# Relu attention pass: rounds written out, the mask added on VectorE, high key parts written by ScalarE and full keys by VectorE from one bank

## The reference

```python
def _L1_xattn_ref(input, context, context_mask, W, b):
    q = jax.nn.relu(jnp.einsum('bih,oh->bio', input, W) + b)
    k = jax.nn.relu(jnp.einsum('bjh,oh->bjo', context, W) + b)
    scores = jnp.einsum('bid,bjd->bij', q, k)
    scores = jnp.where(context_mask[:, None, :], -jnp.inf, scores)
    probs = jax.nn.softmax(scores, axis=2)
    return jnp.einsum('bij,bjd->bid', probs, k)
```

## Time and profile before

| what | value |
|---|---|
| three runs | 1555.84, 1556.08, 1556.17 us |
| the profiled execution | 1554.04 us, its span from first to last instruction 1552.3 us |
| TensorE busy | 1461.3 us (94%), weight loads 1258.2 us |
| VectorE, ScalarE, GpSimd busy | 1080.9, 828.1, 604.7 us |
| granted TensorE clock, mean | 0.975 |

### The profile page before, as it was taken

How to read it: one execution, slowest core, us unless ns; L and a number is a source line. 1 busy time by engine, 2 the same in 40 slices (tenths; PEclk the granted TensorE clock), 3 DMA queues, 4 the chain that set the end, 5 groups by cost and what they waited for, 6 DMA issues and landing times. The chain is left out here.

```text
span 1552.3 us, 24869 instructions
## 1 busy us (share of the span) xinstructions
PE 1461.3 (94%) x9105; PEld 1258.2 (81%) x9105; DVE 1080.9 (70%) x2053; ACT 828.1 (53%) x1578; POOL 604.7 (39%) x519
## 2 busy tenths in 40 slices
PE   6999999999999999999999999999977889999379
PEld 5888888888888888888888888888865778888248
DVE  6777777777777777777777777777775356666764
ACT  2655665556665565665565666565651255555121
POOL 6343433434343434343434343433300256665330
PEclk9999999999999999999999999999997899999779
DMA  5000000000000000000000000000007112220600
GB/s 183 1 8 18 1 25 1 25 1 25 1 25 1 25 1 25 1 24 1 24 1 24 1 24 1 1 1 1 1 28 312 63 70 71 71 71 24 284 1 4
DMA packets 9102, 57.18 MB, mean 37 GB/s; under 512 B 2121, under 2 KB 2720, under 8 KB 7969
## 3 DMA queue, kind: packets, MB, share of 16 engines
q1 hardware_dynamic: 8992, 55.73, 9.6%
HBM read 55.60 MB, written 0.13 MB: 36 GB/s over the span
## 5 line engine op out<-in xcount | busy, mean ns | idle before, releaser
L468 DVE TENSOR_TENSOR pT<-ps,pT 128x896 fp32r<-128x896 f32 x224 | 244.5, 1092 | 204.2 <-ACT pT L378 204.2
L305 POOL CAST V<-Vraw 128x512 fp32r<-128x512 f32 x189 | 115.8, 613 | 653.1 <-ACT Vraw L384 552.3
L378 ACT ACTIVATE pT<-ps 128x896 fp32r<-128x896 f32 x224 | 206.1, 920 | 179.1 <-PE ps L540 178.3
L384 ACT COPY Vraw<-ps 128x512 f32<-128x512 f32 x189 | 111.0, 587 | 265.3 <-PE ps L522 265.3
L306 POOL TENSOR_TENSOR V<-Vraw,V 128x512 fp32r<-128x512 f32 x189 | 242.3, 1282 | 15.1
L422 DVE TENSOR_REDUCE nmx<-ps 128x1 f32<-128x896 f32 x224 | 242.0, 1080 | 0.0
L365 ACT ACTIVATE prob<-ps,nm 128x896 f32<-128x896 f32 x224 | 224.2, 1001 | 0.0
L598 PE MATMUL ps<-ident,prob 128*128 128x128 f32 x1568 | 214.5, 277 | 8.6 <-ACT prob L365 4.5
L553 PEld LDWEIGHTS ps<-pT,V 128*128 128x128 f32 x1568 | 215.0, 188 | 8.3 <-issue 0.3
L553 PE MATMUL ps<-pT,V 128*128 128x256 f32 x1568 | 220.2, 280 | 0.0
L598 PEld LDWEIGHTS ps<-ident,prob 128*128 128x128 f32 x1568 | 167.5, 140 | 17.1 <-ACT prob L365 9.2
(11 more groups left out here) (307 smaller groups left out, 2398.6 us busy)
## 6 DMA issues: line engine op xcount, KB each, us to landing
raw<-in_ctxT SPq DMA_DIRECT2D x14, 896.0 KB, 4.5
d_raw<-in_ctxT SPq DMA_DIRECT2D x14, 896.0 KB, 4.6
w<-in_w SPq DMA_DIRECT2D x2, 4096.0 KB, 18.3
wg<-in_wg SPq DMA_DIRECT2D x1, 4352.0 KB, 27.5
wu<-in_wu SPq DMA_DIRECT2D x1, 4352.0 KB, 16.8
wd<-in_wd SPq DMA_DIRECT2D x1, 4352.0 KB, 26.7
e_ea<-in_alog SPq DMA_DIRECT2D x1, 2048.0 KB, 7.3
wq<-in_wq SPq DMA_DIRECT2D x1, 1024.0 KB, 5.3
```

Source lines behind the costliest of these rows:

```text
L305: link(pool, nc.gpsimd.tensor_copy(v_high(g, i), by_head(Vraw[:, j % 2, :])), "pool_chain")
L378: nc.scalar.activation(pT[u % 2][:, :, 0, :], pT_ps, ACT.Copy).then_inc(sem("pTh_ready"), 1)
L468: nc.vector.tensor_tensor(pT[u % 2][:, :, 1, :], pT_ps, pT[u % 2][:, :, 0, :].bitcast(F32), ALU.subtract).then_inc(sem("pTl_ready"), 1)
```

## The change

- The full keys are no longer ScalarE's. ScalarE writes the high part `d_kTh` straight from the bank, with bias and Relu (`keys`, `dkTh_ready`). VectorE then reads the same bank, adds the bias, takes the maximum with 0 and writes the full keys `d_kT` (`keys_full`, `dkT_ready`). The key groups' wait for their bank is still on `dkT_ready`, now VectorE's.
- The mask is loaded as 128 equal rows. VectorE adds mask times -1e30 to the scores as it reads them from the banks and writes `d_Sm` in SBUF; the maximum and the exponentials read `d_Sm`. The two mask products, `mneg` and the row of ones are gone.
- The scores of a half wait for the key parts of that half only, and go half by half.
- The high and low parts of the context and the full keys have two buffers each. Chunks 1 and 2 are both split ahead of round 0 (ScalarE) and in it (GpSimd), the others one round earlier than their keys, as before.
- The loops are gone: all 14 rounds are written out in each queue.
- `du_free` starts at 1, and `exp_step(c)` asks for c + 1.
- `wg` is allocated after the pass and loaded in `stage_scan`.

With `groups_ahead` = 4 the list `done` is 4, 8, ... 56, so each round still makes the four groups of the next chunk.

```diff
@@ -135,12 +135,14 @@
         keep("br1", [P, E1])
         with ExitStack() as experts:
 
-            v["wg"] = sb("wg", [P, KT, EA * F1], F32, experts)
             with ExitStack() as second:
 
-                v["d_raw0"] = sb("d_raw0", [P, KT, CK], F32, second)
-                for name, width in (("d_cTh", CK), ("d_cTl", CK), ("d_wxh", D), ("d_wxl", D)):
-                    v[name] = sb(name, [P, KT, width], F32R, second)
+                v["d_raw"] = [sb(f"d_raw{i}", [P, KT, CK], F32, second) for i in range(2)]
+                v["d_cTh"] = [sb(f"d_cTh{i}", [P, KT, CK], F32R, second) for i in range(2)]
+                v["d_cTl"] = [sb(f"d_cTl{i}", [P, KT, CK], F32R, second) for i in range(2)]
+                v["d_kT"] = [sb(f"d_kT{i}", [P, KT, CK], F32, second) for i in range(2)]
+                v["d_wxh"], v["d_wxl"] = (sb(name, [P, KT, D], F32R, second) for name in ("d_wxh", "d_wxl"))
+                v["early_groups"], v["early_splits"], v["early_loads"], v["groups_ahead"] = 0, 1, 1, 2 * KT
...
+            v["wg"] = sb("wg", [P, KT, EA * F1], F32, experts)
...
                 sp.dma_start(ea[:, :], t["alog"].partition_broadcast(P)).then_inc(sem("alog_in"), 16)
+                sp.dma_start(v["wg"][:, :, :], t["wg1"]).then_inc(sem("mix1_in"), 16)
                 sp.dma_start(v["wu"][:, :, :], t["wu1"]).then_inc(sem("mix1_in"), 16)
                 sp.dma_start(v["wd"][:, :, :], t["wd1"]).then_inc(sem("wd_in"), 16)
...
-    last = chunks // 2 - 1
+    KG = 2 * KT
+    NG = (NT + 1) // 2
+    groups = KG * chunks
+    early, split = v["early_groups"], v["early_splits"]
+    ahead = v["groups_ahead"]
+    done = [max(early, ahead)]
+    for c in range(chunks):
+        left = chunks - 1 - c
+        share = -(-(groups - done[-1]) // left) if left > 0 else 0
+        done.append(done[-1] + share)
+
+    def first_use(C):
+
+        return next((c for c in range(chunks) if done[c + 1] > KG * C), None)
+
+    to_split = {c: [C for C in range(chunks) if KG * C >= done[0] and max(first_use(C) - 1, 0) == c]
+                for c in range(chunks)}
...
+        Sm = sb("d_Sm", [P, 2, HK], F32, own)
...
+                def load_mask(c):
+                    if c >= 2:
+                        sp.wait_ge(sem("dmasked"), c - 1)
+                    sp.dma_start(mrow[c % 2][:, :], t["mask"][c].partition_broadcast(P)).then_inc(
+                        sem(f"dmask_in{c % 2}"), 16)
+
+                load_mask(0)
+                load_mask(1)
+                masks = 2
+                for C in range(v["early_loads"], chunks):
+                    if C >= 2:
+                        sp.wait_ge(sem("dcTl_ready"), C - 1)
+                    sp.dma_start(raw[C % 2][:, :, :], t["ctxT"][C]).then_inc(sem(f"dctx_in{C % 2}"), 16)
+                    if C >= 2 and masks < C - 1:
+                        load_mask(masks)
+                        masks += 1
+                for c in range(masks, chunks):
+                    load_mask(c)
...
+                def keys_low(c, g):
+                    pool.wait_ge(sem("dkT_ready"), KG * c + g + 1)
+                    nc.gpsimd.tensor_tensor(part(kTl, g), part(kT[c % ring], g), part(kTh, g).bitcast(F32),
+                                            ALU.subtract).then_inc(sem("dkTl_ready"), 1)
+
                 norm_pool(pool, 3)
+                for C in range(split, (done[0] + KG - 1) // KG):
+                    split_low(C)
                 for g in range(KG):
+                    keys_low(0, g)
+                for c in range(chunks):
+                    if c == 0:
+                        for C in to_split[0]:
+                            split_low(C)
+                    if c + 1 < chunks:
                         for g in range(KG):
+                            keys_low(c + 1, g)
+                    for C in to_split[c]:
+                        if c > 0:
+                            split_low(C)
 
...
-                def keys(g):
-                    nc.scalar.activation(part(kT, g), ps[:, g % 2, 0:HK], ACT.Relu, bias=bx[:, g // 2:g // 2 + 1],
-                                         scale=1.0).then_inc(sem("dkT_ready"), 1)
...
+                def keys(G):
+                    C, g = G // KG, G % KG
+                    act.wait_ge(sem("dk_done"), G + 1)
+                    if C >= 1:
+                        act.wait_ge(sem("ds_done"), C)
+                        act.wait_ge(sem("dkTl_ready"), KG * C)
+                    nc.scalar.activation(part(kTh, g), ps[:, G % 2, 0:HK], ACT.Relu, bias=bx[:, g // 2:g // 2 + 1],
+                                         scale=1.0).then_inc(sem("dkTh_ready"), 1)
+
+                def split_high(C):
+                    act.wait_ge(sem(f"dctx_in{C % 2}"), 16 * (C // 2 + 1))
+                    if C >= 2:
+                        act.wait_ge(sem("dk_done"), KG * (C - 1))
+                    nc.scalar.copy(cTh[C % 2][:, :, :], raw[C % 2][:, :, :]).then_inc(sem("dcTh_ready"), 1)
+
...
+                def exp_step(c):
+                    b = c % 2
+                    act.wait_ge(sem("dmax_done"), c + 1)
+                    act.wait_ge(sem("du_free"), c + 1)
+                    nc.scalar.activation(al[:, b:b + 1], nm[:, 1 - b:2 - b], ACT.Exp, bias=nm[:, b:b + 1], scale=-1.0)
+                    nc.scalar.activation(prob[:, :, :], Sm[:, :, :], ACT.Exp, bias=nm[:, b:b + 1], scale=1.0,
+                                         accum_out=rs[:, b:b + 1]).then_inc(sem("dexp_done"), 1)
 
...
+                for G in range(before, done[0]):
+                    keys(G)
+                for C in to_split[0]:
+                    split_high(C)
...
-                            act.wait_ge(sem("dmax_done"), i * 2 + (b + 2))
-                            act.wait_ge(sem("du_free"), i * 2 + (b + 2))
-                            exp_step(1 - b)
...
+                    for G in range(done[c], done[c + 1]):
+                        keys(G)
+                    if c > 0:
+                        for C in to_split[c]:
+                            split_high(C)
+                    for n in range(2):
+                        act.wait_ge(sem("dp_turned"), 2 * c + n + 1)
+                        nc.scalar.copy(pTh[:, turned_cols(n)], ps[:, 4 + n, 0:len(PG[n]) * P]).then_inc(sem("dpTh_ready"), 1)
+                    if c + 1 < chunks:
+                        for n in range(NG):
+                            rows_high(c + 1, n)
+                        exp_step(c + 1)
 
...
-                nc.vector.memset(nm[:, :], BIG).then_inc(sem("du_free"), 2)
+                nc.vector.memset(nm[:, :], BIG).then_inc(sem("du_free"), 1)
...
-                def keys_high(g):
-                    nc.vector.tensor_copy(part(kTh, g), part(kT, g)).then_inc(sem("dkTh_ready"), 1)
...
+                def keys_full(c):
+                    if c >= ring:
+                        dve.wait_ge(sem("dk_turned"), NG * (c - ring + 1))
+                        dve.wait_ge(sem("dkTl_ready"), KG * (c - ring + 1))
+                    for g in range(KG):
+                        G = KG * c + g
+                        dve.wait_ge(sem("dkTh_ready"), G + 1)
+                        nc.vector.tensor_scalar(part(kT[c % ring], g), ps[:, G % 2, 0:HK], bx[:, g // 2:g // 2 + 1], 0.0,
+                                                ALU.add, ALU.max).then_inc(sem("dkT_ready"), 1)
+
...
+                def masked_max(c):
+                    b = c % 2
+                    dve.wait_ge(sem(f"dmask_in{b}"), 16 * (c // 2 + 1))
+                    dve.wait_ge(sem("ds_done"), c + 1)
+                    if c >= 1:
+                        dve.wait_ge(sem("dexp_done"), c)
+                    nc.vector.scalar_tensor_tensor(Sm[:, :, :], mrow[b][:, :].rearrange("p (a n) -> p a n", a=2), -BIG, S,
+                                                   ALU.mult, ALU.add).then_inc(sem("dmasked"), 1)
+                    dve.wait_ge(sem("dmasked"), c + 1)
+                    nc.vector.tensor_reduce(nmx[:, :], Sm[:, :, :], mybir.AxisListType.XY, ALU.max,
+                                            negate=True).then_inc(sem("dchunk_max"), 1)
+                    dve.wait_ge(sem("dchunk_max"), c + 1)
+                    nc.vector.tensor_scalar(nm[:, b:b + 1], nmx[:, :], nm[:, 1 - b:2 - b], None,
+                                            ALU.min).then_inc(sem("dmax_done"), 1)
+
+                keys_full(0)
                 for n in range(NG):
                     rows_low(0, n)
...
+                def turn_keys(c, n):
+                    pe.wait_ge(sem("dkT_ready"), KG * (c + 1))
...
-                def scores(b, low_parts):
+                def scores(c):
                     halves = [slice(half * HK, (half + 1) * HK) for half in range(2)]
+                    if c >= 1:
+                        pe.wait_ge(sem("dmasked"), c)
                     for half, cols in enumerate(halves):
-                        nc.tensor.matmul(S[:, half, :], one_b[:, :], mneg[b][:, cols], start=True, stop=False)
```

(36 more changed lines are left out.)

307 lines of the change are left out of this document (94 added, 213 removed).

## The result

The changed kernel took 1575.11 us (median of four runs, 1572.84 to 1584.60), the kernel before 1556.12 us beside it (four runs, 1555.84 to 1556.85): a ratio of 1.0133 with a 95% interval of 1.0101 to 1.0164. It is slower, as forecast; the forecast was 1579 us. The profiled execution took 1572.84 us with a span of 1571.1 us, 18.8 us above the span before.

What follows compares the result with a forecast made beforehand. TensorE's order was taken to bound the kernel. Rounds 13.2, head 5.1 and tail 4.7 us sum to 23.0; 1554.04 + 23.0 + 2.04 gives 1579 us, range 1568 to 1594.

Steps and rivals of the forecast that it cites:

- x: Price of VectorE's write of full keys from the bank: between 0.37 and 1.23 us, taken as 0.61.
- twelve rounds more: Rounds of 14.82 us, 1.13 above 13.69; twelve give 13.6, less six loop ends of 0.07: 13.2 us.
- head: Start of the pass: round 0 begins 3.8 us late and takes 1.3 us more, 5.1 us in all.
- tail: End of the pass: 2.6 us waiting for the exponentials plus 2.1 us for an assumed half clock, 4.7 us.
- The bank's path: VectorE's full-key write now frees the bank; alone, scores at +7.57 against +7.64, gain eaten to 0.07 us a round.
- +6.35: Scores' start in a round without the two mask products and the wait before them: at most 1.29 us gained.
- The new wait: Exponentials wait for the present chunk's U update, ending at +2.73 in the next round; the round becomes 14.82 us.
- At nothing: Moved wg load, 128-row masks, GpSimd's low key parts, dmasked and the kT ring were to cost nothing.
- The rule on loops: Six loop ends at 0.07 us give 0.4 us; the skill's rule alone would have written-out rounds gain more.
- The wait did not hide: Rival: the exponentials' wait hides, rounds stay even, only head and part of the tail count: +5, 1561 us; chance 0.07.
- the clock kept 1.00: Rival: TensorE's clock falls every round because of its new idle gaps: +17, 1596 us; chance 0.13.
- the bank's write was not 0.37 us: Rival, faster: VectorE writes full keys at 0.37 us and U's wait hides: 1552 us; chance 0.05.

Runs made afterwards that it cites:

- a1: Changed kernel with du_free starting at 2 again, so the exponentials wait only for the U update of the chunk before: 1559.94 us, ratio 1.0032.
- c1: a2 with TensorE waiting for all four parts of d_kTh before the scores: 1550.91 us, ratio 0.9965.
- a2: Changed kernel with du_free at 2 again, ScalarE writing full keys from the bank and VectorE copying high parts: 1541.47 us, ratio 0.9917.
- a0: The changed kernel run once more, with no edit: 1574.63 us, ratio 1.0116 to the kernel before.
- d1: a1 with TensorE turning probabilities between second and third key groups, and the scores' high part before the first turning of keys: 1552.26 us.
- e2: d1 with ScalarE's and VectorE's copies of the turned probabilities also moved between the second and third group: 1547.42 us, ratio 0.9948.
- b1: Kernel before with only du_free starting at 1, so the exponentials wait for the present chunk's U update: 1559.80 us, ratio 1.0029.

## Why the prediction was right, point by point

| term | forecast, us | measured, us |
|---|---|---|
| x, VectorE's full part | 0.61 | 0.68 |
| third group | +4.12 | +4.14 |
| scores | +8.80 | +8.77 |
| round | 14.82 | 14.80 (mean 14.77) |
| twelve rounds more | 13.2 | 13.05 |
| head | 5.1 | 3.1 |
| tail, wait and half clock | 2.6 + 2.1 | 2.7 + 1.9 |
| after the pass | 0 | -2.0 |
| sum on the profile | 23.0 | 18.8 |

The twelve rounds measured are from the start of round 1 (1275.01, before near 1271.9) to where the last turning of probabilities stood ready (1455.06 less its wait of 2.72, before 1436.18): 177.33 against 164.28. The tail's 1.9 us is what is left of the pass's 20.8 us.

- **The bank's path** held. The price x was 0.68, near the row of L415 and far from both ends of the fast and slow copies; it never left 674 to 685 ns. The 0.07 us too little in the first part was made up by ScalarE, whose exponentials and first high part, one right behind the other, ended at +3.27 and not at +3.41. That this path alone leaves the round as before (+7.57 against +7.64) is what a1 shows: 13.67 against 13.69. But it is a sum of two things that I had netted, and c1 and a2 take them apart: the halves are worth 0.78 us, everything else that a2 keeps of the change (masks, second buffers, written-out rounds, low parts half by half) 0.42, the bank's path costs 1.19. The prediction has no word on the halves at all: its +6.35 leaves out the wait for the fourth copy, which is right for a2 only because of them. My step "the scores could begin about +6.35" was the start of a2, 1.2 us a round that I gave away as eaten without naming it as a kernel of its own.
- **The new wait** held in mechanism and size, and a1 shows it by its absence: 1.10 us a round, where ScalarE had been released by `d_U` thirteen times. What the sum had wrong beside it is small: it takes the six loop ends off the twelve rounds, but the 13.69 that it compares with has them in already. Twelve times 1.13 is 13.6 and not 13.2. And the rounds before are 13.66 and 13.71 us in turn, so that a loop end is 0.05 us and not 0.07.
- **The head** is the term mis-sized: 3.1 for 5.1. Round 0 started at 1258.59 and not 1260.7, 2.1 us early, and then took 16.4 us for the 16.3 forecast. Of the 2.1 us 0.9 were there when the scores began (1255.37 for 1256.3; third group 1247.40 for 1247.67). The other 1.2 are the clock's: I let its half cover all twelve score products, and in this execution the first six went at the full clock, their loads at 0.39 us a pair, and the slow ones (0.56 a pair) began at 1256.50. In a0 the fall came earlier and cost more, a first U 31.6 us behind `d_qT` for 30.6.
- **The tail** held: 2.72 us of wait, then a granted clock of 0.57 from 1454 to 1462, with seven turnings in 1.35 us for 0.79.
- **At nothing.** `wg`, the masks, GpSimd: right. What I had not counted is that the later pass was followed by shorter stages, 2.0 us. In the first products of the mixture, 1.3 us, it is the granted clock, which came back sooner; for the rest no run tells.
- **The rule on loops.** For the loop ends I kept 0.4; no run here undoes only the writing out. All that c1 keeps of the change gives 0.42 us a round, and the two mask products that went took 0.53 us by themselves. The Trainium skill's rule (Runtime: NRT & Kernel Launch, Instruction fetch mechanics) is that a taken branch out of the fetched pages stalls; as far as that difference tells, there was no such stall to gain back in this kernel.
- **The rivals.** The wait did not hide; the clock kept 1.00 in the middle of the pass although TensorE idled 1.8 us and 1.0 us in each round; the bank's write was not 0.37 us. The forecast of slower came true by the way given; the 4 us by which it was too high are 2.0 us in the head and 2.0 in the stages behind the pass.

## What to carry to other kernels

A start value of a semaphore is a piece of the schedule: with one slot fewer, an engine that has its data waits for the end of the round before, and everything queued behind it waits too. What that costs depends on the rest: 1.1 to 1.2 us a round with the pass for the mask on VectorE, nothing on average in the kernel before. Moving a write to a second engine behind the first puts both in series on the buffer's release, and that is paid where TensorE's order has no other work at those two places; covering them moved the waits elsewhere (d1) until the other engines' orders were changed too (e2). When several edits come in one change, price each alone before netting them: here one part of the edits was worth 1.2 us a round and two others cost 2.3.

## What the runs showed that I had not expected

- VectorE's copy of a part of keys within SBUF takes 0.37 to 1.38 us for the same shape, by what GpSimd does beside it, while its write from the bank took 0.674 to 0.685 us in 56 of 56. In a2 the four copies of a round last 0.39, 0.76, 1.01 and 1.27 us, the later ones beside GpSimd's subtractions (1.15 us each). The Trainium skill, SBUF — State Buffer, Who interferes with whom, says that such copies can take a pair of ports shared with GpSimd, and that whichever of the two starts first has it for its whole length. The trace of b1 agrees: the copy that starts first takes 0.39 us and the subtraction beside it 1.37 to 1.39, and where the subtraction starts first it takes 1.14 to 1.15 us and the copy 1.37 to 1.38. By the same section a write from a bank is outside of it, as measured. So the change did make VectorE's part steadier, and its mean shorter than the copies before (0.68 against 0.76 us), only in the wrong place.
- In b1 a wait of 0.41 us in a round made seven rounds shorter, 13.3 for 13.7 us, and five longer, 14.2, as it put the fourth copy a few nanoseconds ahead of GpSimd's subtraction or behind it.
